# Layer 2 attention of a four-layer kernel: probabilities turned in 32x32 blocks by VectorE, value products in four row tiles, one batch behind the scores

## The chip, the core and the metric

The kernel runs on one core of one Trainium2 chip as one program. The metric is the device time of that program in microseconds (us), median over runs. TensorE (PE) multiplies matrices into PSUM, which has 8 banks; VectorE (DVE), ScalarE (ACT) and GpSimd (POOL) work element by element; SyncE (SP) issues the DMA transfers. The engines run their own instruction streams in program order and wait for each other by semaphores.

## What is computed

The program is a stack of four layers, each an attention over a context of 1500 rows and a feed-forward part. Only the attention of the third (numbered 2) is changed. Its reference, with 16 batches, 56 queries, 1500 context rows, 16 heads of 64:

```python
xn = _ln(x, ln1_s, ln1_b);  cn = _ln(context, lnc_s, lnc_b)
q = xn @ Wq
k, v = jnp.split(cn @ Wkv, 2, axis=-1)
k = jnp.concatenate((nk, k), axis=2)      # one null key and one null value in front
v = jnp.concatenate((nv, v), axis=2)
sim = jnp.where(mfull, jnp.einsum('bhid,bhjd->bhij', q * scale, k), max_neg)
attn = jax.nn.softmax(sim, axis=-1)
out = jnp.einsum('bhij,bhjd->bhid', attn, v)
out = out.transpose(0, 2, 1, 3).reshape(b, n, h * d) @ Wo
return _ln(out, lno_s, lno_b)
```

## The kernel before

All of the stage is float32. The weights are folded first, so that queries and values meet the normalised context itself: `QZ` holds per batch 16 heads x 56 queries = 896 query rows of 128 features, which are seven **tiles** of 128 rows (`RT = 7`), 112 tiles in all. The 128th feature row stands for the null key. The context lies in 12 chunks of 125 rows (`NCH`, `CH`).

For a tile m of batch b = m // 7 the work is a chain over four engines:

- PE, `scores(m, c)`, line 1611: three products of the tile with 501 keys each, into three of six PSUM banks, two tiles in turn.
- DVE, `maximum(m)`, line 1823: adds the mask `MA`, takes the row maximum and writes the sum to SBUF (`SM`).
- ACT, `exp(m)`, line 1751: exponential into `PR` with the row sums. DVE, `scale(m)`, lines 1830 and 1832: reciprocal of the sum, and `PR` times it.
- PE, `unit("T", m, j)`, line 1625: twelve transposes of 126 columns, four to a bank, in the last two banks in turn; three copies take them to SBUF as `PT` (DVE line 1800, ACT line 1740).
- PE, `unit("O", m, 0)`, line 1630: twelve products of a 125-key chunk of `V` with 128 columns of `PT`, summed in one bank; ACT copies the result over the tile's rows in `QZ` (line 1742).

The order is written out by hand in each engine's loop over n: `scores(n + 2, c)` stand between the three groups of transposes of tile n, and the value products of tile n-1 behind them. `WideHeadUnits` numbers these units and gives each of them its bank and the copy it has to wait for.

Once per batch the keys of the next one are loaded transposed (`load_keys`), together with their means and scales spread over all partitions, and POOL normalises them in place (lines 1725 and 1728). The keys of batch 0 come from PE transposes instead (line 1638). The values are loaded plain (`RAW`), and DVE normalises them in twelve instructions (line 1813). ACT makes the next batch's mask (line 1758). After the last tile the products with `WVO` follow (line 1704), a layer norm and the residual sum.

Two short pieces of other stages are read in the prediction: line 498, the value products of layers 0 and 3, which already run in four column tiles (`tile_position=(0, 32 * g)`: 128 input rows, 32 output rows each), and line 1044, a product with 56 input rows between products with 125 and 112 (lines 1043 and 1033).

Of the kernel before, what the change touches and what calls it, by code (L numbers as in the profile page):

```python
# [8 lines left out]
U8 = mybir.dt.uint8  # L9
# [4 lines left out]
P = 128  # L14
# [1380 lines left out]
RT = 7  # L1395
NPR = 501


class WideAhead:
# [3 lines left out]
    SEMS = "w_loaded rows_loaded products scaled centred summed ve_ready spread"  # L1403

    def __init__(self, ctx, nc, k, src):
# [5 lines left out]
        self.WORK = sb("work", [P, 2, 2, 2048])  # L1411
# [4 lines left out]
        self.W = self.WORK[0:HD].rearrange("p a b n -> p (a b) n").rearrange("p m (h n) -> p m h n", h=H)  # L1416
# [30 lines left out]
    def variances(self):  # L1447
        self.nc.vector.tensor_scalar(self.rs[:], self.k.ctx_mv[:, :, :, 1], 1e-6, None, ALU.add).then_inc(self.s.ve_ready, 1)
# [12 lines left out]
class WideHeadUnits:  # L1461


    def __init__(self):
        self.units = [("K", 0, j, "D") for j in range(3)]
        self.last_step = RT * B + 1
        for n in range(self.last_step + 1):
            self.units += [u for u in (self.first(n), self.second(n), self.third(n), self.output(n)) if u]
        self.place = {u[:3]: i for i, u in enumerate(self.units)}
        self.count = []  # L1470
        seen = {"A": 0, "D": 0}
        for u in self.units:
            seen[u[3]] += 1
            self.count.append(seen[u[3]])

    def first(self, n):
        return ("T", n, 0, "D") if n < RT * B else None

    def second(self, n):
        return ("T", n, 1, "A") if n < RT * B else None  # L1480

    def third(self, n):
        return ("T", n, 2, "A") if n < RT * B else None

    def output(self, n):
        return ("O", n - 1, 0, "A") if 0 <= n - 1 < RT * B else None

    def filled(self, *what):
        return self.place[what] + 1

    def bank(self, *what):
        return 6 + self.place[what] % 2

    def emptied(self, *what):
        i = self.place[what]
        return self.units[i][3], self.count[i]

    def before(self, *what):
        i = self.place[what] - 2
        return (self.units[i][3], self.count[i]) if i >= 0 else None  # L1500


def attention_16_wide_heads(nc, k, src, ahead):
# [7 lines left out]
    D, A = "D", "A"  # L1511
    plan = WideHeadUnits()
    with ExitStack() as ctx:
# [3 lines left out]
                       "ctx_loaded0 ctx_loaded1 mask_loaded0 mask_loaded1 null_rows constants mask_ready "  # L1517
                       "v_ready moments_filled moments_ready moments_stored slot_ready key_parts keys_moved keys_scaled filled emptied_a emptied_d scores_filled max_done exp_done rinv_ready scaled out_filled out_ready "
                       "dve_chain")
        s2 = semaphores(ctx, nc, name + "o", LN_SEMS)  # L1520
        ctx_loaded = (s.ctx_loaded0, s.ctx_loaded1)
        mask_loaded = (s.mask_loaded0, s.mask_loaded1)
# [5 lines left out]
        RAW = sb("raw", [CH, 2, NCH, P])  # L1528
        V = sb("values", [CH + 1, 2, NCH, P])
        KT = sb("keys", [P, 2, S2 + 1])  # L1530
        MR = sb("mask", [P, 2, S2], U8)
        MA = sb("maskadd", [P, 2, 3, NPR])
        PT = sb("probsT", [CH + 1, 2, NCH, P])
        OUT = sb("out", [P, TOK])
        MOMENTS = sb("moments", [B // 2 * NCH, 4, CH])
# [5 lines left out]
        SCALE_OF = WQK[:].rearrange("p h n -> p (h n)")[:, 0:S2]  # L1541
        PR = WORK[:, 0].rearrange("p a n -> p (a n)")[:, 0:2 * 3 * NPR].rearrange("p (u n) -> p u n", u=2)
        SM = WORK[:, 1].rearrange("p a n -> p (a n)")[:, 0:2 * 3 * NPR].rearrange("p (u n) -> p u n", u=2)
        tile_rows = lambda m: QZ[:, m // RT, m % RT * P:(m % RT + 1) * P]
        heads_of = lambda b, h: QZ[:, b, h * Q:(h + 1) * Q]
        half = lambda x, h: QZ[:, 8 * x:8 * x + 8, h * Q:(h + 1) * Q]
        keys_in = lambda c: CH + 1 if c == NCH - 1 else CH

        def wait_emptied(eng, which):
            e, n = which  # L1550
            eng.wait_ge(s.emptied_a if e == A else s.emptied_d, n)

        def wait_context(eng, b):
            eng.wait_ge(ctx_loaded[b % 2], 16 * (b // 2 + 1))

        def wait_mask(eng, b):
            eng.wait_ge(mask_loaded[b % 2], 16 * (b // 2 + 1))
# [4 lines left out]
        def _(sp):  # L1562
            def load_context(b):
                if b >= 2:
                    sp.wait_ge(s.v_ready, 3 * b - 3)
                sp.dma_start(RAW[:, b % 2], src["ctx"][b]).then_inc(ctx_loaded[b % 2], 16)

            def load_mask(b):
                if b >= 2:
                    sp.wait_ge(s.mask_ready, b - 1)  # L1570
                sp.dma_start(MR[:, b % 2, :], src["mask_full"][b].partition_broadcast(P)).then_inc(mask_loaded[b % 2], 16)

            load_context(0)
            for u in range(2):
                sp.dma_start(V[CH:CH + 1, u, NCH - 1, :], k.ident[P - 1:P, :]).then_inc(s.null_rows, 16)
            def load_keys(b):
                if b == 1:
                    sp.wait_ge(s.slot_ready, 2)
                    sp.wait_ge(s.q_filled, 2 * H)
# [1117 lines left out]
```

## Time and profile before

| | us |
|---|---|
| median of 3 runs | 2212.78 (2210.36 to 2214.6) |
| span of the profiled execution | 2210.2 |
| layer 2 attention, first scores to the products with `WVO` | 896.5 to 1636.5 |
| PE busy over the span | 2062.2 (93%) |
| DVE, ACT, POOL busy over the span | 1482.6, 1200.2, 752.7 |

The profile is of one execution, whose span runs from its first to its last instruction; the runs have no such span, so the median is set beside it. A float32 product shows in the trace as two records, each with a weight load of its own: called passes here; a transpose is one. PE's records overlap, since products are pipelined: how long one occupies the engine is read from the distance between starts, not from its duration.

### The profile page before, as it was taken

What the parts mean: (1) busy time and instruction counts of PE and PEld (TensorE: products, weight loads), DVE (VectorE), ACT (ScalarE), POOL (GpSimd) and SP (SyncE); (2) the same over time, 40 slices, a digit from 0 to 9 for tenths busy, and PEclk for the clock granted to TensorE, in tenths of its full rate; (3) what the DMA queues carried; (4) which work ended last, traced back from release to release, by engine and by line L of the source; (5) the groups of instructions that cost most, each with busy time, mean ns of one, the idle gap of its engine ahead of it and who ended that gap; (6) DMA issues with size and microseconds to landing.
All of it is one profiled execution on the core that took longest, in us unless ns stands there. A gap on an engine that the chain in (4) does not pass through costs nothing. (4 is left out here: it accounts for less than half of the span.)

```text
span 2210.2 us, 47308 instructions
## 1 busy us (share of the span) xinstructions
PE 2062.2 (93%) x18797; PEld 1505.9 (68%) x18797; DVE 1482.6 (67%) x3068; ACT 1200.2 (54%) x2313; POOL 752.7 (34%) x337
## 2 busy tenths in 40 slices
PE   5999999866999899999999999999997799999996
PEld 3677777655887455677777777777764457777774
DVE  5677777688986554566666666666626577777774
ACT  5877887634766222344444444444421467777763
POOL 6565566016875470112111211112000254433410
PEclk8999999967999898999999999999997889999997
DMA  6554544233540311231112211131000354544420
GB/s 161 148 148 132 159 134 132 63 85 97 143 136 20 79 38 39 70 104 66 60 60 82 97 60 60 60 100 62 1 1 25 87 159 126 149 126 139 122 79 9
DMA packets 94541, 199.78 MB, mean 90 GB/s; under 512 B 42113, under 2 KB 50353, under 8 KB 94066
## 3 DMA queue, kind: packets, MB, share of 16 engines
q1 hardware_dynamic: 94322, 196.75, 30.3%
q8 instruction: 151, 2.47, 0.5%
q14 instruction: 68, 0.56, 0.1%
HBM read 116.22 MB, written 0.65 MB: 53 GB/s over the span
## 5 line engine op out<-in xcount | busy, mean ns | idle before, releaser
L1630 PEld LDWEIGHTS L2ps<-L2probsT,L2values 125*128 125x128 f32 (+1 forms) x2688 | 317.4, 192 | 51.3 <-issue 48.9
L1611 PE MATMUL L2ps<-L2keys,L2qz 128*128 128x501 f32 x672 | 340.2, 590 | 0.9 <-DVE L2out_bias L1847 0.9
L1630 PE MATMUL L2ps<-L2probsT,L2values 125*128 125x128 f32 (+1 forms) x2688 | 318.5, 275 | 0.5 <-ACT L2probsT L1740 0.5
L1725 POOL TENSOR_TENSOR L2keys<-L2keys,L2mean_spread 127x1500 f32<-127x1500 f32 x15 | 50.9, 3395 | 583.0 <-DMA L2wqk<-L_moments 583.0
L1823 DVE CUSTOM_DVE_ANT_0 L2work<-L2ps,L2maskadd,L2big 128x1503 f32<-128x1503 f32 x112 | 199.5, 1781 | 72.9 <-PE L2ps L1611 72.7
L1625 PEld LDWEIGHTS L2ps<-const,L2work 128*126 128x126 f32 x1344 | 164.3, 140 | 118.7 <-issue 116.5
L654 ACT ACTIVATE L3probsT<-L3ps 128x448 f32<-128x448 f32 x384 | 196.0, 547 | 71.1 <-PE L3ps L511 66.5
L654 ACT ACTIVATE L0probsT<-L0ps 128x448 f32<-128x448 f32 x384 | 198.1, 551 | 47.7 <-PE L0ps L511 46.6
L1625 PE MATMUL L2ps<-const,L2work 128*126 128x128 f32 x1344 | 202.8, 273 | 3.5 <-DVE L2work L1832 3.1
L1742 ACT COPY L2qz<-L2ps 128x128 f32<-128x128 f32 x112 | 29.7, 265 | 304.7 <-PE L2ps L1630 304.7
L798 DVE TENSOR_REDUCE L0partmax<-L0ps 112x1 f32<-112x1000 f32 x128 | 153.4, 1199 | 58.1 <-PE L0ps L484 56.0
L798 DVE TENSOR_REDUCE L3partmax<-L3ps 112x1 f32<-112x1000 f32 x128 | 153.4, 1199 | 58.1 <-PE L3ps L484 56.0
L1751 ACT ACTIVATE L2work<-L2work,L2negmax 128x1503 f32<-128x1503 f32 x112 | 173.9, 1553 | 16.9 <-DVE L2negmax L1823 16.8
L1740 ACT COPY L2probsT<-L2ps 126x512 f32<-126x512 f32 x224 | 130.7, 585 | 77.2 <-PE L2ps L1625 77.2
L1800 DVE COPY L2probsT<-L2ps 126x512 f32<-126x512 f32 x112 | 77.4, 691 | 134.4 <-PE L2ps L1625 134.3
L511 PEld LDWEIGHTS L0ps<-L0query_stack,L0key_stack 99*128 99x128 bf16 x1536 | 110.3, 99 | 57.2 <-issue 13.3
L511 PEld LDWEIGHTS L3ps<-L3query_stack,L3key_stack 98*128 98x128 bf16 x1536 | 110.3, 99 | 54.5 <-issue 13.6
L1832 DVE TENSOR_SCALAR L2work<-L2work,L2rinv 128x1503 f32<-128x1503 f32 x112 | 138.2, 1234 | 3.9
L511 PE MATMUL L0ps<-L0query_stack,L0key_stack 99*128 99x112 bf16 x1536 | 133.5, 214 | 1.3 <-ACT L0probsT L654 1.3
L511 PE MATMUL L3ps<-L3query_stack,L3key_stack 98*128 98x112 bf16 x1536 | 133.1, 214 | 0.0
L605 POOL TENSOR_TENSOR L3keys<-L3keys,L3key_parts 128x1500 f32<-128x1500 f32 x16 | 48.5, 3034 | 192.9 <-ACT L3key_parts L701 192.9
L793 DVE TENSOR_REDUCE L0partmax<-L0ps 112x1 f32<-112x500 f32 x128 | 86.2, 674 | 33.2 <-PE L0ps L476 33.2
(479 smaller groups left out, 4164.7 us busy)
## 6 DMA issues: line engine op xcount, KB each, us to landing
L0key_stack<-L0key_parts SPq DMA_DIRECT2D x192, 187.5 KB
L3key_stack<-L3key_parts SPq DMA_DIRECT2D x192, 187.5 KB
L0ctxT<-in_ctxT SPq DMA_DIRECT2D x16, 750.0 KB, 4.4
L1rawT<-in_ctxT SPq DMA_DIRECT2D x16, 750.0 KB, 6.5
L2raw<-in_ctx SPq DMA_DIRECT2D x16, 750.0 KB
L3ctxT<-in_ctxT SPq DMA_DIRECT2D x16, 750.0 KB, 4.4
L2mean_spread<-L_moments SPq DMA_DIRECT2D x15, 750.0 KB, 6.7
L2wqk<-L_moments SPq DMA_DIRECT2D x15, 750.0 KB, 8.4
```

The lines of the kernel that those rows point to most:

```text
L511: last = nc.tensor.matmul(PS[:, bank, c * TT:(c + 1) * TT], KS[:, h % 4, tau, key_columns(4 * j + c)], QS[:, h % 4, tau, :], start=True, s ...
L654: ins = nc.scalar.activation(PT[:, h % 2, 4 * j:4 * j + 4, tau, :], PS[:, bank, 0:HALF].rearrange("p (c n) -> p c n", c=4), ACT.Exp)
L793: nc.vector.tensor_reduce(PM[:, h % 2, tau, 0:1], PS[0:TT, 0, 0:500], AX.X, ALU.max).then_inc(s.m0_done, 1)
L798: nc.vector.tensor_reduce(PM[:, h % 2, tau, 1:2], PS[0:TT, 1:3, 0:500], AX.XY, ALU.max).then_inc(s.m12_done, 1)
L1611: last = nc.tensor.matmul(PS[:, 3 * (m % 2) + c, 0:NPR], tile_rows(m), KT[:, m // RT % 2, 500 * c:500 * c + NPR], start=True, stop=True)
L1625: last = nc.tensor.transpose(PS[0:CH + 1, bank, c * P:(c + 1) * P], PR[:, i % 2, at:at + CH + 1], k.ident)
L1630: last = nc.tensor.matmul(PS[:, bank, 0:P], V[0:keys_in(c), i // RT % 2, c, :], PT[0:keys_in(c), i % 2, c, :], start=c == 0, stop=c == NCH ...
L1740: ins = nc.scalar.copy(PT[:, i % 2, 4 * j:4 * j + 4, :].rearrange("p c n -> p (c n)"), PS[0:CH + 1, bank, :])
L1751: nc.scalar.activation(PR[:, m % 2, :], SM[:, m % 2, :], ACT.Exp, bias=nmax[:, m % 4:m % 4 + 1], scale=-1.0, accum_out=ssum[:, m % 4:m % 4 ...
L1800: ins = nc.vector.tensor_copy(PT[:, i % 2, 4 * j:4 * j + 4, :].rearrange("p c n -> p (c n)"), PS[0:CH + 1, bank, :])
L1823: nc.vector.tensor_tensor_reduce(SM[:, m % 2, :].rearrange("p (c n) -> p c n", c=3), PS[:, 3 * (m % 2):3 * (m % 2) + 3, 0:NPR], MA[:, m // ...
L1832: nc.vector.tensor_scalar(PR[:, m % 2, :], PR[:, m % 2, :], rinv[:, m % 4:m % 4 + 1], None, ALU.mult).then_inc(s.scaled, 1)
```

## The change

Only `attention_16_wide_heads` and the small class `WideAhead`, which prepares for it, are touched; `WideHeadUnits` goes.

- The 1500 keys are no longer met in three runs of 501 but in four **windows** of 12 x 32: window w takes from each chunk of 125 its keys 32w to 32w+31 (`key_window`), so a row of probabilities is 48 blocks of 32 (1536 columns; those past a chunk's end are masked, and the null key has one of them). The four products of a tile fill banks 0 to 3, for all tiles from the ninth on.
- `scale` moves from DVE to ACT, `exp` works in place, and DVE turns the tile's probabilities in 32x32 blocks from SBUF to SBUF in one instruction (`turn`). So the block's 32 keys lie on the 32 partitions of the quadrant that held 32 of the tile's query rows. `PT` holds a whole batch turned.
- The value products (`weigh`) run once over a whole batch: for each of 48 blocks, four products, one on each quadrant of 32 partitions (`tile_position=(a * 32, 0)`), with 224 columns (seven tiles x 32 query rows), into banks 4 to 7. Their values `V` lie in all four quadrants, so each row is loaded four times. Seven steps of seven blocks (the last of six) stand behind the scores, eight tiles later (`LAG`). ACT empties the four banks once per batch (`take_heads`).
- The values are normalised on POOL, 12 instructions a window with means and scales from `VST`, and are single: the next batch's windows are loaded as the steps let go of them. The keys of batch 0 are loaded and normalised as all others are.

```diff
-NPR = 501
+WINDOWS = 4
+BW = 32
+BLOCKS = WINDOWS * NCH
+NPR = BLOCKS * BW
+LAG = RT + 1
...
+        score_bank = lambda m: 4 if m < LAG and m % 2 else 0
...
+            return KEYS[:, at:at + NCH * CH].rearrange("p (c n) -> p c n", n=CH)[:, :, 0:BW]
...
+            def load_values(b, w):
+                if b:
+                    last_step = (NCH * w + NCH - 1) // RT
+                    sp.wait_ge(s.pv_done, RT * (b - 1) + last_step + 1)
...
+                for a in range(4):
+                    sp.dma_start(V[a * BW:a * BW + n, w * NCH:(w + 1) * NCH, :], src["ctx"][b][w * BW:w * BW + n]
+                                 ).then_inc(values_loaded[w], 16)
...
+            for b in range(B):
+                if b + 1 < B:
+                    load_keys(b + 1)
+                    load_moments(b + 1)
+                    load_mask(b + 1)
+                if b:
+                    for w in range(WINDOWS):
+                        load_values(b, w)
...
+            def scores(m):
+                b = m // RT
+                if m > LAG:
+                    pe.wait_ge(s.max_done, m)
+                elif m >= 2:
+                    pe.wait_ge(s.max_done, m - 1)
+                if m % RT == 0:
+                    pe.wait_ge(s.keys_scaled, b + 1)
+                for w in range(WINDOWS):
+                    last = nc.tensor.matmul(PS[:, score_bank(m) + w, 0:NCH * BW], tile_rows(m), key_window(b, w), start=True, stop=True)
+                last.then_inc(s.scores_filled, 1)
+
+            def weigh(step):
+                b, g = divmod(step, RT)
+                if g == 0:
+                    pe.wait_ge(s.turned, RT * b + RT)
+                    if b:
+                        pe.wait_ge(s.heads_ready, 4 * b)
...
+                blocks = step_blocks(g)
+                pe.wait_ge(s.v_ready, WINDOWS * b + blocks[-1] // NCH + 1)
+                for n in blocks:
+                    for a in range(4):
+                        last = nc.tensor.matmul(PS[:, 4 + a, 0:RT * BW], V[a * BW:(a + 1) * BW, n, :], block_cells(a, b, n),
+                                                start=n == 0, stop=n == BLOCKS - 1, tile_position=(a * BW, 0))
+                last.then_inc(s.pv_done, 1)
...
-            for j in range(3):
-                unit("K", 0, j, D)
...
+            for n in range(1, TILES + LAG):
+                if n < TILES:
+                    scores(n)
+                if n >= LAG:
+                    weigh(n - LAG)
...
+            def normalise_values(b, w):
+                pool.wait_ge(values_loaded[w], 64 * (b + 1))
+                blocks = slice(w * NCH, (w + 1) * NCH)
+                nc.gpsimd.tensor_copy(V[:, blocks, P - 1:P], NULL[:, blocks].unsqueeze(2))
+                for c in range(NCH):
+                    x = V[:, w * NCH + c, 0:P - 1]
+                    last = nc.gpsimd.tensor_scalar(x, x, VST[:, 0, w, b, c:c + 1], VST[:, 1, w, b, c:c + 1],
+                                                   ALU.subtract, ALU.mult)
+                last.then_inc(s.v_ready, 1)
...
+            def scale(m):
+                act.wait_ge(s.rinv_ready, m + 1)
+                nc.scalar.mul(SM[:, m % 2, 0:NPR], SM[:, m % 2, 0:NPR], rinv[:, m % 4:m % 4 + 1]).then_inc(s.scaled, 1)
+
+            def take_heads(b):
+                act.wait_ge(s.pv_done, RT * b + RT)
+                for a in range(4):
+                    nc.scalar.copy(by_quadrant(b)[:, :, a, :], PS[:, 4 + a, 0:RT * BW].rearrange("p (t n) -> p t n", n=BW)
+                                   ).then_inc(s.heads_ready, 1)
...
+            for n in range(TILES + LAG):
+                b, t = divmod(n, RT)
+                if n < TILES:
+                    exp(n)
+                if n >= LAG and (n - LAG) % RT == RT - 1:
+                    take_heads((n - LAG) // RT)
+                if n < TILES:
+                    scale(n)
...
+            def turn(m):
+                b, t = divmod(m, RT)
+                dve.wait_ge(s.scaled, m + 1)
+                if b:
+                    dve.wait_ge(s.pv_done, RT * (b - 1) + t + 1)
+                nc.vector.transpose(turned_cells(b, t), SM[:, m % 2].rearrange("p (g r n) -> p g r n", g=RT, n=BW)
+                                    ).then_inc(s.turned, 1)
...
+            for n in range(TILES + 1):
+                if n < TILES:
+                    maximum(n)
+                if n:
+                    turn(n - 1)
+                if n < TILES:
+                    invert(n)
```

PE before, from the end of the folding into the loop of tiles and one period of it (`L2work` holds the probabilities, `L2values` the values or, at line 1638, the keys' source):

```order
L1676 MATMUL L2ps<-L2bias_heads,L2work 128x1 x16
L1638 MATMUL L2ps<-const,L2values 128x125 x11
L1638 MATMUL L2ps<-const,L2values 128x126
L1611 MATMUL L2ps<-L2keys,L2qz 128x501 x6
L1625 MATMUL L2ps<-const,L2work 126x128 x4
L1611 MATMUL L2ps<-L2keys,L2qz 128x501
```

PE after, at the same place (line 1615 is `scores`, line 1631 `weigh`):

```order
L1664 MATMUL L2ps<-L2work 128x128 x16
L1670 MATMUL L2ps<-L2bias_heads,L2work 128x1 x16
L1615 MATMUL L2ps<-L2keys,L2qz 128x384 x36
L1631 MATMUL L2ps<-L2work,L2values 128x224 x28
L1615 MATMUL L2ps<-L2keys,L2qz 128x384 x4
```

The transposes are gone, nine tiles of scores stand ahead of the first value products, and from there 4 products of scores and 28 of values alternate.

DVE before, one tile in the middle of a batch that has a part of the next batch's values to normalise (`ISA` is the instruction of `maximum`):

```order
L1800 COPY L2probsT<-L2ps 126x512
L1813 TENSOR_SCALAR L2values<-L2raw,ctx_mv,L2rs 125x127 x4
L1830 RECIPROCAL L2rinv<-L2sums 128x1
L1832 TENSOR_SCALAR L2work<-L2work,L2rinv 128x1503
L1823 ISA L2work,L2negmax<-L2ps,L2maskadd,L2big 128x1503
L1823 ISA L2negmax 128x1
```

DVE after, one tile (the turn is of the tile before):

```order
L1806 ISA L2work,L2negmax<-L2ps,L2maskadd,L2big 128x1536
L1806 ISA L2negmax 128x1
L1816 STREAM_TRANSPOSE L2work<-L2work 128x49x32
L1821 RECIPROCAL L2rinv<-L2sums 128x1
L1806 ISA L2work,L2negmax<-L2ps,L2maskadd,L2big 128x1536
```

The copy, the scaling and the values have left DVE; the turn has come.

POOL after, one batch (before, the first two rows were all that stood here; `L2wqk` holds the scales):

```order
L1697 TENSOR_TENSOR L2keys<-L2keys,L2mean_spread 127x1500
L1699 TENSOR_TENSOR L2keys<-L2keys,L2wqk 127x1500
L1704 COPY L2values<-L2null_column 128x12
L1707 TENSOR_SCALAR L2values<-L2values,L2value_stats 128x127 x12
L1704 COPY L2values<-L2null_column 128x12
```

The last two kinds come four times a batch, behind the keys of the next one.

## Rows read from the trace of the kernel before

**Rows 1.** Stretches: us, engines' busy us (instructions), PE clock, DMA share, GB/s.

```profile
894.00:898.00 4.00, 3.13 (x10) 1.79 (x9) 1.94 (x4) 0.00 (x0) 0.98 (x1) 0.50 0.46 169
1000.00:1100.00 100.00, 100.00 (x645) 77.26 (x644) 67.19 (x105) 47.01 (x79) 14.68 (x4) 1.00 0.20 66
```

**Rows 2.** Timeline of PE, one tile: start us, us, line, operation, count.

```profile
1203.47 2.84 PE L1630 MATMUL L2ps<-L2probsT,L2values 125*128 125x128 f32 x24
1206.15 0.60 PE L1625 MATMUL L2ps<-const,L2work 128*126 128x128 f32 x4
1206.59 1.01 PE L1611 MATMUL L2ps<-L2keys,L2qz 128*128 128x501 f32 x2
...
1209.99 2.84 PE L1630 MATMUL L2ps<-L2probsT,L2values 125*128 125x128 f32 x24
```

**Rows 3.** Groups by line, 900 to 1630: count, busy us, mean ns, idle before.

```profile
L1823 DVE CUSTOM_DVE_ANT_0 L2work<-L2ps,L2maskadd,L2big 128x1503 f32<-128x1503 f32 x112 | 199.5, 1781 | 72.9 <-PE L2ps L1611 72.7
L1751 ACT ACTIVATE L2work<-L2work,L2negmax 128x1503 f32<-128x1503 f32 x112 | 173.9, 1553 | 16.9 <-DVE L2negmax L1823 16.8
...
L1832 DVE TENSOR_SCALAR L2work<-L2work,L2rinv 128x1503 f32<-128x1503 f32 x112 | 138.2, 1234 | 3.9
L1740 ACT COPY L2probsT<-L2ps 126x512 f32<-126x512 f32 x223 | 130.1, 585 | 77.0 <-PE L2ps L1625 76.9
...
L1813 DVE TENSOR_SCALAR L2values<-L2raw,ctx_mv,L2rs 125x127 f32<-125x127 f32 x180 | 49.7, 340 | 0.0
...
L1742 ACT COPY L2qz<-L2ps 128x128 f32<-128x128 f32 x110 | 29.2, 265 | 300.1 <-PE L2ps L1630 300.1
L1758 ACT ACTIVATE L2maskadd<-L2mask,L2big 128x1500 f32<-128x1500 uint8 x15 | 23.3, 1551 | 0.0
...
L1830 DVE RECIPROCAL L2rinv<-L2sums 128x1 f32<-128x1 f32 x112 | 17.9, 160 | 48.0 <-ACT L2work L1751 47.9
```

**Rows 4.** Timeline of PE in layer 0, four column tiles and what follows.

```profile
151.84 0.78 PE L498 MATMUL L0ps<-L0probsT,L0values 128*32 128x112 f32 x24
152.55 0.42 PE L484 MATMUL L0ps<-L0key_stack,L0query_stack 97*112 97x500 bf16 x1
```

**Rows 5.** Timeline of PE in layer 1, a 56-row product between others.

```profile
575.47 2.79 PE L1043 MATMUL L1ps<-L1raw,L1probsT 125*112 125x128 f32 x24
578.19 0.47 PE L1044 MATMUL L1ps<-L1v_latents,L1probsT 56*112 56x128 f32 x2
578.59 1.56 PE L1033 MATMUL L1ps<-const,L1probs 112*125 112x112 f32 x12
579.99 0.26 PE L1036 MATMUL L1ps<-const,L1probs 112*56 112x112 f32 x1
```

**Rows 6.** Groups by line on POOL, whole span.

```profile
L609 POOL TENSOR_SCALAR L0key_parts<-L0keys 128x1500 bf16<-128x1500 f32 x15 | 59.9, 3994 | 2.9 <-POOL L0keys L605 2.9
...
L1728 POOL TENSOR_TENSOR L2keys<-L2keys,L2wqk 127x1500 f32<-127x1500 f32 x15 | 58.4, 3892 | 1.2
L1725 POOL TENSOR_TENSOR L2keys<-L2keys,L2mean_spread 127x1500 f32<-127x1500 f32 x15 | 50.9, 3395 | 583.0 <-DMA L2wqk<-L_moments 583.0
...
L1722 POOL COPY L2keys<-const 128x1 f32<-128x1 f32 x1 | 0.2, 187 | 0.1
```

**Rows 7.** Issues of transfers, 830 to 1640: count, KB each, median us to landing.

```profile
L2mean_spread<-L_moments SPq DMA_DIRECT2D x15, 750.0 KB, 6.7
```

**Rows 8.** Timeline of PE at the start of the stage.

```profile
889.47 3.63 PE L1676 MATMUL L2ps<-L2bias_heads,L2work 64*128 64x1 f32 x32
893.03 2.64 PE L1638 MATMUL L2ps<-const,L2values 125*128 125x125 f32 x12
896.54 7.12 PE L1611 MATMUL L2ps<-L2keys,L2qz 128*128 128x501 f32 x12 [0.87 <-DVE L2out_bias L1847]
```

**Rows 9.** Instructions of a line: count, ns min/median/max, first and last start.

```profile
L1823 DVE CUSTOM_DVE_ANT_0 L2work<-L2ps,L2maskadd,L2big x112: 1768/1783/1784, 901.3 to 1620.9; 128x1503 f32<-128x1503 f32 x112
L1704 PE MATMUL L2ps<-L2qz,L2wvo x64: 539/539/644, 1636.5 to 1660.3; 128*128 128x448 f32 x64
```

More of the change, by code:

```diff
@@ L1458, in vector @@
                                 ).then_inc(s.summed, 1)
[L1461 to L1500, printed above, removed]
 def attention_16_wide_heads(nc, k, src, ahead):
@@ L1527, in attention_16_wide_heads @@
         BIG = sb("big", [P, 1])
[L1528 to L1535, printed above, removed]
+        V = sb("values", [P, BLOCKS, P])
+        NULL = sb("null_column", [P, BLOCKS])
+        VST = sb("value_stats", [P, 2, WINDOWS, B, NCH])
+        KEYS = sb("keys", [P, 2 * KEY_COLUMNS + (WINDOWS - 1) * BW - 3])
+        MR = sb("mask", [P, S2], U8)
+        MA = sb("maskadd", [P, 2, WINDOWS, NCH, BW])
         MEAN = sb("mean_spread", [P, S2])
@@ L1549, in wait_emptied @@
[L1549 to L1557, printed above, removed]
+        by_quadrant = lambda b: QZ[:, b].rearrange("p (t a n) -> p t a n", a=4, n=BW)
+        score_bank = lambda m: 4 if m < LAG and m % 2 else 0
+        KT = KEYS[:, 0:2 * KEY_COLUMNS].rearrange("p (u n) -> p u n", u=2)
@@ L1593, in _ @@
             sp.wait_ge(s.moments_stored, 16)
-            load_keys(1)
-            for b in range(2, B):
-                load_context(b)
-                load_mask(b)
-                load_keys(b)
+            load_moments(0)
+            for x, of in enumerate((ahead.means, rs)):
+                for w in range(WINDOWS):
+                    n = BW if w < WINDOWS - 1 else LAST_KEYS
+                    for a in range(4):
+                        sp.dma_start(VST[a * BW:a * BW + n, x, w], of[w * BW:w * BW + n]).then_inc(s.stats_spread, 16)
@@ new lines, in _ @@
+            nc.gpsimd.memset(BIG[:], FLT_MAX).then_inc(s.constants, 1)
+            for u in range(2):
+                nc.gpsimd.memset(MA[:, u, WINDOWS - 1, :, LAST_KEYS:BW], FLT_MAX).then_inc(s.margins, 1)
+            for u in range(2):
+                pool.wait_ge(s.margins, u + 1)
+                nc.gpsimd.memset(MA[:, u, WINDOWS - 1, NCH - 1, LAST_KEYS:LAST_KEYS + 1], 0.0).then_inc(s.margins, 1)
+            pool.wait_ge(s.margins, 4)
+            normalise_keys(0)
+            pool.wait_ge(s.stats_spread, 16 * 2 * WINDOWS * 4)
@@ L1730, in _ @@
+            pool.wait_ge(s.null_column, 2)
+            pool.wait_ge(s.null_rows, 64)
+            for b in range(B):
+                if b + 1 < B:
+                    normalise_keys(b + 1)
+                for w in range(WINDOWS):
+                    normalise_values(b, w)
             ln_pool(pool, k, s2)
```

298 lines of the change are left out of this document (114 added, 184 removed).

## The prediction

> **What bounds the kernel now.** I read the table of stretches first. In the middle of the stage [rows 1] PE is busy for all of the 100 us at a granted clock of 1.00 (2.4 GHz), VectorE for 67, ScalarE for 47, POOL for 15: nothing keeps PE waiting, so the stage lasts as long as PE's instructions do. The timeline of PE gives the period of a tile [rows 2]: value products begin at 1203.47 and again at 1209.99, 6.52 us. Of this the 24 value passes take 2.68 (1203.47 to 1206.15), three groups of four transposes 0.44 each (1206.15 to 1206.59), and three pairs of score passes the rest, 2.52, so 0.84 a pair. 112 periods are 730 of the stage's 740 us. The groups by line say what the others do in a period [rows 3]: DVE 1.78 for the maximum, 1.23 for the scaling, 0.16 for the reciprocal; ACT 1.55 for the exponential.
>
> **PE after.** A pass of 128 columns takes 2.68/24 = 0.1117 us, one of 501 columns 0.42 [rows 2]; the line through both is 0.0059 + 0.000827 per column. So a pass of 384 columns takes 0.323, and the eight of a tile's scores 2.59 (before 2.52). One of 224 columns takes 0.191. The twelve transposes (1.32) go, and nothing else on PE waited for them.
>
> A step of value products is 28 products, 56 passes: 14 rounds of four row tiles. If four tiles run side by side, a round takes 0.191 and a step 2.67; the seventh step of a batch, with six blocks, 2.29. Row tiles aren't in this trace; the nearest are column tiles [rows 4]: 24 passes of 112 columns take 0.71 us to the start of what follows. One after the other, at 0.0985 each by the line, they would take 2.36, so a round costs 0.118 or less. I take full overlap, since this is the nearest row, and keep no overlap (0.764 a round) as the far end.
>
> Going into tiles and out again costs something too. In layer 1 [rows 5] two products of 56 rows stand between wider ones: from 575.47 to 579.99 are 38 passes in 4.52 us, which at 0.110 each would be 4.18, so 0.34 for in and out. From the column tiles it would be 0.71 - 6 x 0.0985 = 0.12. I take 0.35 a step. The period is 2.59 + 2.67 + 0.35 = 5.61 us, 5.23 with the short step, 5.56 on the mean, and 38.9 a batch.
>
> **DVE and ACT.** `maximum` grows from 1503 to 1536 columns, 1.82 us [rows 3]. The copy (0.69) and the scaling go. `turn` is not in the trace: 1568 columns, SBUF to SBUF. At the rate of the scaling it takes 1.29, at that of the maximum 1.86, at twice that 3.7. I take 1.86, the slower of the two that show. With 0.16 for the reciprocal a tile costs DVE some 3.95 us with gaps. ACT has the exponential 1.59, the scaling, a pass of the same length, 1.59, a seventh of a mask (1.55) and of four copies of 224 columns. A copy of 512 takes 0.585, one of 128 0.265 [rows 3], so one of 224 takes 0.345, four 1.4: some 3.6 with gaps. Both lie under 5.56.
>
> The waits: `scores(n+1)` wants `maximum(n)`, 1.82 after the scores, which the step of 3.0 covers. `turn(n-1)` waits for `weigh(n-8)`, since it writes over the cells which that step has read; behind it queue `invert(n)` and `maximum(n+1)`. It starts when the step ends and takes 1.86 + 0.16 while PE does scores for 2.59: 0.6 to spare. The banks 4 to 7 are emptied when the last step of a batch ends; ACT begins when its exponential is done, 1.82 + 1.78 after the scores' end, and copies until 5.0, where PE wants the banks at 5.2. That has the least slack; if it fails, a few tenths a batch are lost, 5 us in all.
>
> **POOL, SP and transfers.** Per batch POOL has the keys, 3.40 + 3.89 [rows 6] and a little, 7.4, and now 48 normalisations of 127 columns and four small copies (0.2). Line 609, the same operation on 1500 columns, takes 3.99, 2.66 ns a column, so 0.34 for 127; a small instruction costs 0.19 [rows 6]. I take 0.53. The bounds are 0.25 (the rate of line 1725 and nothing more) and 0.87 (a pass for each of its two operations). At 0.53 a batch costs 7.4 + 4 x (0.2 + 12 x 0.53) = 33.6 us, under 38.9, so PE hides it; from 0.64 a normalisation POOL is the bound. The Trainium skill, "GPSIMD Engine Reference", section 4.1 Engine selection, calls GpSimd roughly line-rate on operations with one tensor input and about two times slower than VectorE on those with two. By that a normalisation would take what it takes DVE at line 1813, 0.34 [rows 3], and POOL 24.5 us a batch; line 609 has one tensor input and takes more for a column than line 1725 with two, so here the row speaks against the page, and I keep 0.53.
>
> Values are now loaded four times, 3.1 MB a batch, and 5.6 MB in all: 144 GB/s over 38.9 us where 66 are moved now at a DMA share of 0.20 [rows 1]. A window is let go by a step of one batch and needed by the same step of the next or one before, over 27 us later; its loading takes some 7 [rows 7] and its normalising 6.6. SP issues 21 transfers a batch in place of 6. So I cost these at nothing; the cover is those 27 us. The keys of the next batch stand on SP behind the last window of the batch before, and on POOL behind its normalisation, and are still done well inside the batch.
>
> **Start and end.** Without the transposes of the keys the first scores begin at 893.0, not 896.5 [rows 8]. The clock there is 0.50, 1.2 GHz [rows 1]: six passes of 501 until the first maximum at 901.3 [rows 9] took 4.76, so eight of 384 take 4.86, and the first maximum starts at 897.9. Until the first value step, eight tiles later, DVE is the bound at 3.95 a tile: `maximum(7)` starts at 925.5 and ends at 927.4, `turn(6)` ends at 929.3, `weigh(0)` at 932.3. If the clock stays at 0.50 here, PE takes 5.2 a tile and 7 us are lost. Then 103 periods of 5.556 end at 1504.8. The last tile's turn ends at 1510.3 (scores, maximum, exponential, scaling, turn in a row), the last batch's 96 rounds take 18.3 more, the copies 1.4, and the products with `WVO` start at about 1530.5 where they start at 1636.5 now [rows 9]. That is 106 us less: span 2104.2. The median of the runs is 2.6 above the span of the profiled execution, so **2107**. Its own range, from a switch of 0.12 (-26) with a turn of 1.29 at the start (-5), to a lost clock, late copies and tile starts of some hundredths a round, is 2075 to 2135.
>
> **The rivals.**
> - Weight loads of the four row tiles queue up, and the kernel is **slower**. Each product loads 128 columns of weights. The 32 passes with one column [rows 8] take 0.111 us each, so a load is a floor of 0.111, hidden today behind a pass of the same length. Four in a row are 0.444 a round where columns need 0.191. The column tiles don't exclude it: their loads are of 32 columns, and four of a quarter are one of 0.111, within the 0.118 seen. Against it: loads for different rows of the array need not share anything. A batch would take 7 x 2.59 + 96 x 0.444 + 2.45 = 63.2 us, 14.7 batches 357 more, the tail 24: 2488. It decides from a round of 0.26 us, since 1507 rounds (15.7 batches) by 0.07 are the 106 us. Chance 0.14.
> - Tiles overlap less than fully. At a round of 0.25, a third over the columns' time, 1507 x 0.058 = 88: 2195. The Trainium skill, "TensorE: Matmul & The Clock Gate", section Measured speedup vs the span model, has four row tiles of 32 rows at 3.07 times one; by that a round is 0.191 x 4 / 3.07 = 0.249, the same 2195. Rows 4 show more than that for column tiles: 2.36 / 0.71 = 3.3 with the exit included. Chance 0.14.
> - POOL becomes the bound. At 0.87 a batch costs 50 us, 16 of them 800, and the products start near 1701: 2280. From 0.78 it is slower than now. Chance 0.09, of which 0.05 slower.
> - The turn takes 3.7. DVE needs 5.8 a tile, 0.24 over PE, and 15 more at the start: 2150. Chance 0.05.
> - The change doesn't do what it says, and the four row tiles run one after the other: a step is 56 x 0.191 = 10.7, a batch 93.9, some 2970. Chance 0.05.
>
> **How the numbers follow.** The forecast keeps 0.53. About 0.2% is what a measurement of this kernel can tell from no change. Faster: 0.53 + 0.14 + 0.05 + 0.04, less 0.02 for cases that end near the old time, 0.74; slower 0.14 + 0.05 + 0.05 = 0.24. The range reaches from 2075 to POOL's 2280 and leaves out queued loads and no overlap, 0.19.
>
> **What would show it.** In a stretch in the middle PE should be busy throughout, with tiles 5.56 us apart; in a step four passes should start within hundredths of each other and rounds 0.19 apart. A round of 0.44 means queued loads; 0.76 no overlap. POOL should idle some 5 us a batch, `turn` take 1.9 and wait for PE; the first maximum should start near 898 and the products with `WVO` near 1530. PE waiting for values means POOL; PE waiting for the maximum means DVE.

## The result and the profile after

The changed kernel takes 2521.93 us (median of 4 runs, 2518.67 to 2526.13) where the kernel before takes 2213.69 in the same job: 1.1398 times as long, interval 1.138 to 1.1415. The forecast was 2107, in a range of 2075 to 2280. The span of the profiled execution is 2524.3 us.

The products with `WVO` (line 1684 now) begin at 1949.9, where they began at 1636.5 [rows 9]; so all of the loss lies in the stage, as it did in the sum:

```profile
L1684 PE MATMUL L2ps<-L2qz,L2wvo x64: 539/539/643, 1949.9 to 1973.7; 128*128 128x448 f32 x64
```

PE's timeline in the middle of it (start, us, line, operation, count) first shows what was forecast, then a hole:

```profile
1394.51 2.92 PE L1615 MATMUL L2ps<-L2keys,L2qz 128*128 128x384 f32 x8
1397.36 2.93 PE L1631 MATMUL L2ps<-L2work,L2values 32*128 32x224 f32 x56
1400.22 2.92 PE L1615 MATMUL L2ps<-L2keys,L2qz 128*128 128x384 f32 x8
1403.07 2.93 PE L1631 MATMUL L2ps<-L2work,L2values 32*128 32x224 f32 x56
1430.50 4.65 PE L1615 MATMUL L2ps<-L2keys,L2qz 128*128 128x384 f32 x8 [24.50 <-DVE L2negmax L1806]
1435.09 2.93 PE L1631 MATMUL L2ps<-L2work,L2values 32*128 32x224 f32 x56
```

The scores take 2.85 us (1394.51 to 1397.36), the step of values 2.86 (to 1400.22), a tile 5.71. Then, behind the step at 1403.07, PE stands for 24.50 us and comes back at half clock (granted 0.50 from 1431 to 1432): the scores take 4.59. Such a hole comes about once a batch. What PE waited for in the stage (us in total, times, longest):

```profile
PE L2ps L1615 <- DVE L2negmax L1806: 329.8, 16, 25.5
PE L2ps L1631 <- POOL L2values L1707: 36.1, 7, 12.6
PE L2ps L1631 <- DVE L2work L1816: 4.9, 2, 3.2
```

The maximum on DVE is only the last in a row of waits. It stands on DVE behind the reciprocal of the tile before (line 1821 below, idle for 352.1 us), that waits for the exponential on ACT, and ACT stands at the mask of the next batch. So the prediction's sign "PE waiting for the maximum means DVE" misleads here: DVE is busy for only 31.5 of the 100 us from 1400 to 1500. ACT's waits, and its timeline beside PE's hole:

```profile
ACT L2maskadd L1762 <- DMA L2mask<-in_mask_full: 358.3, 14, 28.0
```

```profile
1425.17 1.26 ACT L1762 ACTIVATE L2maskadd<-L2mask,L2big 128x1152 f32<-128x1152 uint8 x1 [26.99 <-DMA L2mask<-in_mask_full]
...
1426.83 1.55 ACT L1744 ACTIVATE L2work<-L2work,L2negmax 128x1536 f32<-128x1536 f32 x1
```

The mask is wanted in the third tile of a batch for the one after, five tiles before its first use, but ACT's stream is in order, and the exponential of the fourth tile stands behind it. So the question is why the mask is late. SP's issues between two batches (the second number is from the issue to SP's next):

```profile
1449.11 3.83 SPq L1552 DMA_DIRECT2D L2values<-in_ctx  x4
1452.98 8.72 SPq L1566 DMA_DIRECT2D L2keys<-in_ctxT  x2
1461.74 0.77 SPq L1574 DMA_DIRECT2D L2mean_spread<-L_moments  x1
1462.55 2.68 SPq L1574 DMA_DIRECT2D L2wqk<-L_moments  x1
1465.27 3.07 SPq L1558 DMA_DIRECT2D L2mask<-in_mask_full  x1
```

The mask goes out 16 us after the last window's values, and lands late on top of that. Issues in the stage, with KB each and the median us to landing:

```profile
L2values<-in_ctx SPq DMA_DIRECT2D x166, 192.0 KB, 3.5
L2wqk<-L_moments SPq DMA_DIRECT2D x13, 750.0 KB, 27.5
L2values<-in_ctx SPq DMA_DIRECT2D x52, 174.0 KB
L2mean_spread<-L_moments SPq DMA_DIRECT2D x12, 750.0 KB, 7.7
L2keys<-in_ctxT SPq DMA_DIRECT2D x12, 656.2 KB, 11.6
L2mask<-in_mask_full SPq DMA_DIRECT2D x13, 187.5 KB, 25.4
L2keys<-in_ctxT SPq DMA_DIRECT2D x12, 87.9 KB, 27.5
```

25 us for 187.5 KB, while 192 KB of values land in 3.5. (The two loads of the keys share a semaphore, and so do means and scales, so the second of a pair tells when both are there.) And the transfers are not short of bandwidth. Stretches (busy time of each engine, then PE's clock, the mean busy share of the 16 DMA engines, GB/s):

```profile
1406.00:1430.50 24.50, 0.00 (x1) 0.00 (x0) 2.00 (x4) 4.89 (x6) 11.30 (x14) 0.59 0.27 77
1450.00:1459.00 9.00, 9.00 (x102) 6.25 (x104) 6.10 (x7) 5.92 (x10) 9.00 (x13) 1.00 0.07 27
1462.00:1468.00 6.00, 6.00 (x66) 4.18 (x65) 3.99 (x5) 1.57 (x1) 1.92 (x3) 1.00 1.03 290
1482.00:1494.00 12.00, 0.00 (x0) 0.00 (x0) 0.00 (x0) 2.64 (x3) 8.57 (x12) 0.50 0.06 26
```

While loads are queued, from 1450 to 1459 and again from 1482 to 1494, the share is 0.06 to 0.07, as much as one engine of sixteen, at 26 to 27 GB/s. Between them, the same queue reaches 290. What keeps one engine busy, the first four runs below did not ask; they went at the mask and at POOL.

The other engines, by line over the stage:

```profile
L1707 POOL TENSOR_SCALAR L2values<-L2values,L2value_stats 128x127 f32<-128x127 f32 x768 | 617.1, 847 | 0.0
...
L1806 DVE CUSTOM_DVE_ANT_0 L2work<-L2ps,L2maskadd,L2big 128x1536 f32<-128x1536 f32 x112 | 203.6, 1818 | 119.1 <-PE L2ps L1615 119.1
L1816 DVE STREAM_TRANSPOSE L2work<-L2work 128x1568 f32<-128x1568 f32 x112 | 202.7, 1810 | 123.1 <-PE L2ps L1631 121.5 <-ACT L2work L1749 1.6
L1749 ACT ACTIVATE L2work<-L2work,L2rinv 128x1536 f32<-128x1536 f32 x112 | 176.8, 1579 | 116.9 <-DVE L2rinv L1821 116.9
...
L1754 ACT COPY L2qz<-L2ps 128x224 f32<-128x224 f32 x64 | 17.1, 349 | 45.3 <-PE L2ps L1631 45.3
L1821 DVE RECIPROCAL L2rinv<-L2sums 128x1 f32<-128x1 f32 x112 | 14.9, 133 | 352.3 <-ACT L2work L1744 352.1
```

### The profile page after: what moved, and what is told of

Same layout as the page of the kernel before. It is cut to its first block and busy times, and to the rows that moved or that the text cites. A ratio compares the mean times of both kernels' runs of the same rounds, so it can differ in the third digit from the quotient of the medians.

```text
span 2524.3 us, 52181 instructions
## 1 busy us (share of the span) xinstructions
PE 2008.6 (80%) x21121; PEld 1411.6 (56%) x21121; DVE 1418.6 (56%) x2765; ACT 1258.0 (50%) x2169; POOL 1368.9 (54%) x1176
## 5 line engine op out<-in xcount | busy, mean ns | idle before, releaser
L1615 PE MATMUL L2ps<-L2keys,L2qz 128*128 128x384 f32 x896 | 360.2, 549 | 330.5 <-DVE L2negmax L1806 329.8
L1707 POOL TENSOR_SCALAR L2values<-L2values,L2value_stats 128x127 f32<-128x127 f32 x768 | 617.1, 847 | 0.0
L1615 PEld LDWEIGHTS L2ps<-L2keys,L2qz 128*128 128x128 f32 x896 | 176.3, 207 | 474.9 <-DVE L2negmax L1806 336.9
L1631 PE MATMUL L2ps<-L2work,L2values 32*128 32x224 f32 x6144 | 334.5, 365 | 41.0 <-POOL L2values L1707 36.1
L1631 PEld LDWEIGHTS L2ps<-L2work,L2values 32*128 32x128 f32 x6144 | 295.4, 192 | 106.3 <-issue 58.8
L1816 DVE STREAM_TRANSPOSE L2work<-L2work 128x1568 f32<-128x1568 f32 x112 | 202.7, 1810 | 123.1 <-PE L2ps L1631 121.5
L1806 DVE CUSTOM_DVE_ANT_0 L2work<-L2ps,L2maskadd,L2big 128x1536 f32<-128x1536 f32 x112 | 203.6, 1818 | 119.1 <-PE L2ps L1615 119.1
L1744 ACT ACTIVATE L2work<-L2work,L2negmax 128x1536 f32<-128x1536 f32 x112 | 176.2, 1573 | 134.9 <-DVE L2negmax L1806 134.7
L1749 ACT ACTIVATE L2work<-L2work,L2rinv 128x1536 f32<-128x1536 f32 x112 | 176.8, 1579 | 116.9 <-DVE L2rinv L1821 116.9
L1821 DVE RECIPROCAL L2rinv<-L2sums 128x1 f32<-128x1 f32 x112 | 14.9, 133 | 352.3 <-ACT L2work L1744 352.1
L1762 ACT ACTIVATE L2maskadd<-L2mask,L2big 128x1152 f32<-128x1152 uint8 x16 | 20.2, 1264 | 358.3 <-DMA L2mask<-in_mask_full 358.3
L605 POOL TENSOR_TENSOR L3keys<-L3keys,L3key_parts 128x1500 f32<-128x1500 f32 x16 | 48.6, 3035 | 195.5 <-ACT L3key_parts L701 195.5
L605 POOL TENSOR_TENSOR L0keys<-L0keys,L0key_parts 128x1500 f32<-128x1500 f32 x16 | 48.6, 3037 | 130.2 <-ACT L0key_parts L701 130.2
## 6 DMA issues: line engine op xcount, KB each, us to landing
L0key_stack<-L0key_parts SPq DMA_DIRECT2D x192, 187.5 KB
L3key_stack<-L3key_parts SPq DMA_DIRECT2D x192, 187.5 KB
```

The costliest lines, as they stand in the source:

```text
L605: nc.gpsimd.tensor_tensor(x, x, parts[:, 0], ALU.subtract).then_inc(s.parts_ready, 1)
L1615: last = nc.tensor.matmul(PS[:, score_bank(m) + w, 0:NCH * BW], tile_rows(m), key_window(b, w), start=True, stop=True)
L1631: last = nc.tensor.matmul(PS[:, 4 + a, 0:RT * BW], V[a * BW:(a + 1) * BW, n, :], block_cells(a, b, n), start=n == 0, stop=n == BLOCKS - 1, ...
L1707: last = nc.gpsimd.tensor_scalar(x, x, VST[:, 0, w, b, c:c + 1], VST[:, 1, w, b, c:c + 1], ALU.subtract, ALU.mult)
L1744: nc.scalar.activation(SM[:, m % 2, 0:NPR], SM[:, m % 2, 0:NPR], ACT.Exp, bias=nmax[:, m % 4:m % 4 + 1], scale=-1.0, accum_out=ssum[:, m % ...
L1749: nc.scalar.mul(SM[:, m % 2, 0:NPR], SM[:, m % 2, 0:NPR], rinv[:, m % 4:m % 4 + 1]).then_inc(s.scaled, 1)
```

## The experiments

**Is it the mask or POOL?** The theory then: ACT stands at the mask, because its load is issued too late on SP and lands 25 us after. The rival: POOL, whose normalising takes 0.80 us (9.61 for twelve), and whose 46 us a batch are more than PE's 39.6. The first run moves the mask's load ahead:

```diff
+            load_mask(1)
             for b in range(B):
                 if b + 1 < B:
                     load_keys(b + 1)
                     load_moments(b + 1)
-                    load_mask(b + 1)
                 if b:
-                    for w in range(WINDOWS):
+                    for w in range(2):
                         load_values(b, w)
+                if b + 2 < B:
+                    load_mask(b + 2)
+                if b:
+                    for w in range(2, WINDOWS):
+                        load_values(b, w)
```

> One part moved: the load of the next batch's mask goes ahead on SP, between two windows of values one batch earlier, where what it waits for is long done; all else as in the changed kernel. Theory (the queue): ScalarE stands 25 us a batch at the mask, because its transfer is issued behind keys, means and scales and lands 25 us after its issue; so the stall goes, 15 x 25 = 375 us at most, and what is late next is POOL, 4 x (0.2 + 12 x 0.80) + 6 to 7 = 46 us a batch where PE needs 39.6: about 2524 - 16 x 20 = 2200, between 2150 and 2290. Rival (POOL): the values' normalising holds the loop already, the mask is late only because the steps are, and the time stays within 2% of 2522.

Measured: 2410.2 us, 1.0882 times the kernel before (1.086 to 1.0904). The wait for the mask is gone but for the first, 8.4 us. Yet only 112 us came back, not 320, so neither the theory's number nor the rival's holds. PE now waits for values and keys:

```profile
PE L2ps L1636 <- POOL L2values L1712: 188.0, 46, 11.8
PE L2ps L1620 <- POOL L2keys L1704: 16.4, 15, 1.9
```

The second run leaves out POOL's normalising, so its values stay as loaded, and keeps SP's order.

```diff
-                nc.gpsimd.tensor_copy(V[:, blocks, P - 1:P], NULL[:, blocks].unsqueeze(2))
-                for c in range(NCH):
-                    x = V[:, w * NCH + c, 0:P - 1]
-                    last = nc.gpsimd.tensor_scalar(x, x, VST[:, 0, w, b, c:c + 1], VST[:, 1, w, b, c:c + 1],
-                                                   ALU.subtract, ALU.mult)
-                last.then_inc(s.v_ready, 1)
+                nc.gpsimd.tensor_copy(V[:, blocks, P - 1:P], NULL[:, blocks].unsqueeze(2)).then_inc(s.v_ready, 1)
```

> The 48 normalising instructions of a batch are left out (the values stay as loaded; the copy of the null column gives the signal), the order on SP is that of the changed kernel. Theory (the queue): POOL idles 20 us of 66 a batch already, so the stall at the mask stays at some 20 to 25 us a batch and only the end of the stage gets shorter, by the 33 us that PE waited there for POOL: 2440 to 2510. Rival (POOL): without its 39 us a batch the loop falls to PE's 39.6 a batch, 2100 to 2150.

Measured: 2500.72 us in one run, as the theory had it. With 38 of POOL's 46 us a batch gone the time falls by 1%, and ACT waits for the mask as before:

```profile
ACT L2maskadd L1757 <- DMA L2mask<-in_mask_full: 374.3, 14, 27.6
```

So POOL does not hold the loop, in spite of its price. The third run moves the other end of the wait, where ACT makes the mask.

```diff
-                if t == 2 and b + 1 < B:
+                if t == 5 and b + 1 < B:
```

> ScalarE makes the next batch's mask after tile 5 of a batch and not after tile 2; SP's order is that of the changed kernel. Theory (the queue): the mask is wanted three periods (3 x 5.70 = 17 us) later, so 17 of the 25 us a batch go, 15 x 17 = 257 less: about 2270, and not under 2200, where POOL's 46 us a batch stand. Rival (POOL): no change, within 2% of 2522.

Measured: 2417.95 us in one run. The direction is the theory's, the size is not: the wait for the mask falls from 358.3 to 50.5 us, but PE waits 192.5 for values and 38.3 for keys instead. From either end, the mask is worth 104 to 112 us, and something else stands right behind it.

The fourth takes the mask early, as in the first run, and the normalising in two operations a window (shown here):

```diff
...
-                for c in range(NCH):
-                    x = V[:, w * NCH + c, 0:P - 1]
-                    last = nc.gpsimd.tensor_scalar(x, x, VST[:, 0, w, b, c:c + 1], VST[:, 1, w, b, c:c + 1],
-                                                   ALU.subtract, ALU.mult)
-                last.then_inc(s.v_ready, 1)
+                x = V[:, blocks, 0:P - 1]
+                of = lambda k: VST[:, k, w, b].unsqueeze(2).to_broadcast([P, NCH, P - 1])
+                nc.gpsimd.tensor_tensor(x, x, of(0), ALU.subtract).then_inc(s.v_moved, 1)
+                pool.wait_ge(s.v_moved, WINDOWS * b + w + 1)
+                nc.gpsimd.tensor_tensor(x, x, of(1), ALU.mult).then_inc(s.v_ready, 1)
```

> The mask's load early as in the first run, and the values of a window normalised by two operations of 12 x 127 columns with means and scales spread by a zero stride, in place of twelve of 127 with two scalars each. The same kind took 3.1 us for 1500 columns at the keys, so 6.4 a window, 26 a batch and 32 with the keys. Theory: POOL falls under PE's 39.6 us a batch and PE is the bound: 2524 - 15 x 27 = about 2120, 2095 to 2160, faster than the kernel before (2213). Rival: the keys' transfers, which land 10 to 28 us after their issue, become the next wait, some 5 to 10 us a batch: 2200 to 2280.

Measured: 2340.49 us, 1.0576 times the kernel before (1.055 to 1.0601). Both numbers missed again. POOL's price fell from 9.6 to 5.5 us a window, and POOL waits where PE's steps need the last window:

```profile
1361.84 2.73 POOL L1714 TENSOR_TENSOR L2values<-L2values,L2value_stats 128x1524 f32<-128x1524 f32 x1
1389.03 0.20 POOL L1709 COPY L2values<-L2null_column 128x12 f32<-128x12 f32 x1 [24.45 <-DMA L2values<-in_ctx]
```

The fourth window's values are issued on SP before 1357 (when the next keys' issue begins) and are there at 1389: over 30 us, where the loads of the other windows land in 3.5. What sets this window apart is 29 rows in place of 32. That was the second theory: **a transfer of 29 rows runs on one DMA engine**. Four of them are 4 x 29 x 6144 bytes = 0.71 MB, at 27 GB/s some 26 us (an estimate), and keys, means, scales and mask, each with a share on that engine, land behind them. Against it: the values are loaded four times, and the queues are simply full.

The fifth run cuts the 29 rows and changes nothing else in the changed kernel, but that POOL waits for the count of eight transfers; the sixth loads 28 of them, in one transfer a quadrant (`LAST_KEYS - 1` in place of `LAST_KEYS` in the first line below).

```diff
-                n = BW if w < WINDOWS - 1 else LAST_KEYS
+                parts = ((0, BW),) if w < WINDOWS - 1 else ((0, 16), (16, LAST_KEYS))
                 for a in range(4):
-                    sp.dma_start(V[a * BW:a * BW + n, w * NCH:(w + 1) * NCH, :], src["ctx"][b][w * BW:w * BW + n]
-                                 ).then_inc(values_loaded[w], 16)
+                    for i, j in parts:
+                        sp.dma_start(V[a * BW + i:a * BW + j, w * NCH:(w + 1) * NCH, :], src["ctx"][b][w * BW + i:w * BW + j]
+                                     ).then_inc(values_loaded[w], 16)
...
-                pool.wait_ge(values_loaded[w], 64 * (b + 1))
+                pool.wait_ge(values_loaded[w], (64 if w < WINDOWS - 1 else 128) * (b + 1))
```

> The changed kernel with one edit: the four loads of the last window (29 rows each) are issued as 16 rows and 13 rows; order, bytes and all other engines stay. Theory (one DMA engine): a transfer of 29 rows runs on one of the 16 DMA engines, at 26 to 28 GB/s with 1.05 engines busy, so the four take 25 us and every later transfer has a share queued behind them; split, they land in 3 to 6 us, the mask about 10 us after its issue, and the wait of ScalarE for it falls from 24 to under 5 us a batch. Then POOL's 46 to 48 us a batch are the bound: 2524 - 15 x 19 = about 2235, between 2180 and 2290. Rival (bytes and issues): the transfers are late because values are loaded four times in many issues; four more issues a batch change nothing or cost 1 to 2 us a batch, 2510 to 2560.

> The changed kernel, but the last window loads 28 of its 29 rows (the 29th key of each chunk's last window keeps value zero), in as many issues and 3% fewer bytes. Theory (one DMA engine): 28 rows are spread over several engines where 29 were not, so the time falls as with the split: 2180 to 2290. Rival (bytes and issues): 2500 to 2525.

Measured: 2199.7 us with the cut, 0.9953 of the kernel before (0.9935 to 0.9971), and 2205.91 in one run with 28 rows. With four more transfers a batch the kernel is 322 us faster, and with 3% fewer bytes in that one window it is 316 faster: the rival is out. The landings with the cut:

```profile
L2wqk<-L_moments SPq DMA_DIRECT2D x11, 750.0 KB, 9.3
L2keys<-in_ctxT SPq DMA_DIRECT2D x11, 656.2 KB, 6.2
...
L2mask<-in_mask_full SPq DMA_DIRECT2D x11, 187.5 KB, 9.2
L2keys<-in_ctxT SPq DMA_DIRECT2D x11, 87.9 KB, 6.7
```

Scales, mask and the small part of the keys fall from 25 to 28 us to 7 to 9, and the mask is in time where the changed kernel has it. What holds this kernel is POOL, as a stretch and the waits of PE show:

```profile
1200.00:1300.00 100.00, 90.49 (x960) 64.12 (x964) 55.41 (x61) 53.63 (x59) 99.84 (x122) 0.95 0.49 135
```

```profile
PE L2ps L1632 <- POOL L2values L1708: 39.4, 15, 3.9
```

**Both together.** The cut, the mask early, the two spread operations:

> The split of the last window's loads, the mask's load early, and the values normalised by two spread operations a window. Theory: with no transfer on a single engine and POOL at 4 x 5.6 + 6 = 29 us a batch, nothing is later than PE, whose period is 5.70 (39.5 a batch): 2340 - 15 x (53 - 39.6) = 2140, less some 10 at the end of the stage: 2105 to 2150, faster than the kernel before (2213). Rival (bytes and issues): it stays at the 2340 of the same kernel without the split.

Measured: 2114.88 us, 0.9556 of the kernel before (0.9539 to 0.9572). In the middle PE is busy throughout at full clock:

```profile
1200.00:1300.00 100.00, 100.00 (x1106) 69.42 (x1100) 64.79 (x72) 63.27 (x70) 71.12 (x35) 1.00 0.62 153
```

```profile
L1690 PE MATMUL L2ps<-L2qz,L2wvo x64: 539/539/643, 1542.9 to 1566.6; 128*128 128x448 f32 x64
```

Between 950 and 1500 PE waits for nothing. The next run has the cut and the two operations with the mask where the changed kernel has it:

> The split and the cheap normalising, with the mask's load where the changed kernel has it, behind keys and means. Theory: the mask is then issued some 5 us after the last window's loads and lands about 12 us later, near the time when ScalarE wants it, so 0 to 5 us a batch are lost against the run with the mask early: 2110 to 2220. Rival (order on SP): the place behind keys and means is enough to stall ScalarE by 10 us or more a batch, 2270 or above.

Measured: 2121.82 us in one run. ACT waits 26.0 us for the mask over the stage. With the cut, the mask's place on SP is worth some 7 us and not 112; the four runs of the kernel with the mask early spread over 9 (2110.04 to 2118.93), so the 7 are hardly clear of them.

**Is it the number of rows?** The fastest kernel with its cut moved:

```diff
-                parts = ((0, BW),) if w < WINDOWS - 1 else ((0, 16), (16, LAST_KEYS))
+                parts = ((0, BW),) if w < WINDOWS - 1 else ((0, 23), (23, LAST_KEYS))
```

> As the fastest run so far (split, mask early, two spread operations a window), but the 29 rows of the last window are cut into 23 and 6 in place of 16 and 13: the same bytes in as many issues. Theory (the engines that a transfer runs on are as many, up to 16, as divide its rows): 23 rows fall on one engine again, 4 x 23 x 6144 bytes at 27 GB/s are 21 us where 29 rows were 27, so most of the loss comes back: 2340 - 15 x 6 = 2250, between 2170 and 2340. Rival (a transfer of more than 16 rows that is no multiple of 16 is slow only as a whole, and any cut mends it): 2105 to 2130, as with 16 and 13.

Measured: 2273.34 us in one run, 158 slower than with 16 and 13. The scales land 27.5 us after their issue again:

```profile
L2wqk<-L_moments SPq DMA_DIRECT2D x10, 750.0 KB, 27.5
...
L2mask<-in_mask_full SPq DMA_DIRECT2D x10, 187.5 KB, 17.0
```

```profile
1352.00:1362.00 10.00, 3.51 (x36) 3.34 (x40) 1.39 (x2) 1.96 (x3) 9.10 (x5) 0.67 0.07 28
```

The last row is a stretch after the last window's loads, columns as above. So cutting as such doesn't help; 28, 16 and 13 rows are fast, 29 and 23 slow. The Trainium skill, "DMA: Bandwidth & Descriptors", section Why a DMA increments its semaphore by 16 and not by 1, gives the rule: a transfer runs on the largest number of engines, up to 16, that divides the size of the slowest dimension on both sides. By it 28 rows get 14, 16 rows 16, 13 rows 13, 29 and 23 rows one. The traces agree: a share of 0.06 to 0.07 and 27 GB/s at 29 rows, 0.07 and 28 at 23, and short landings with 28, 16 and 13.

The number of engines stands in no row, but the pages of the profile count packets. In this order, 29 rows (the changed kernel), 28, 16 and 13 (the cut alone), 23 and 6:

```profile
DMA packets 105520, 240.03 MB, mean 95 GB/s; under 512 B 45689, under 2 KB 54929, under 8 KB 105025
DMA packets 106287, 239.64 MB, mean 109 GB/s; under 512 B 46520, under 2 KB 55760, under 8 KB 105792
DMA packets 107312, 240.04 MB, mean 109 GB/s; under 512 B 47480, under 2 KB 56720, under 8 KB 106816
DMA packets 105899, 239.99 MB, mean 106 GB/s; under 512 B 46072, under 2 KB 55312, under 8 KB 105408
```

A program has 64 of these loads, four in each of 16 batches. Against 29 rows the packets under 512 B are 831, 1791 and 383 more, so 13, 28 and 6 a load; the mask's place and the two operations do not change the count (47480 with all three as well). If every engine of a transfer adds one small packet, which is read from the fit and not shown by itself, and 29 rows have one, then 28 rows have 14, 16 and 13 rows 29, and 23 and 6 rows 7: the rule's numbers.

The page also says that the lowest-numbered engines are taken; by that every other transfer would have a share on the busy one. No run here shows an engine's number, but the single packets in the trace of the changed kernel show such a share: of the 128 packets of the mask that SP issued at 1399.70, 120 start between 1403.4 and 1405.1, and the last eight, a sixteenth, one after another between 1424.2 and 1424.6. ACT, which waits for all of them, goes on at 1425.17.

The last run leaves the normalising out of the kernel with cut and early mask.

> Split and mask early, with the normalising of the values left out altogether (the values stay as loaded). Theory: with two spread operations a window POOL is already hidden and PE is the bound, so the time is that of the run with them, 2105 to 2125. Rival (some of POOL's work is still waited for, or slows VectorE and the transfers while it runs): 2060 to 2100.

Measured: 2110.41 us in one run, inside the spread of the kernel with the two operations (2110.04 to 2118.93): POOL's 29 us a batch are hidden, and PE is the bound.

## Why the prediction was wrong

**The step that failed** is the one on POOL, SP and transfers: "So I cost these at nothing; the cover is those 27 us", with "its loading takes some 7". That 7 was the landing of a transfer of 128 partitions [rows 7], put in place of four of 29. These need some 26 us of one engine by the estimate above, and landed some 35 us after their issue (SP from 1383.22, POOL goes on at 1419.20), so past the cover. And it wasn't the values alone that paid: scales and mask, which SP issued next, landed 25 to 28 us after their issue. The bytes were summed (144 GB/s), but not the engines that carry them. The same sentence passed over the mask. Its load was moved behind keys, means and scales and its buffer halved, ACT wants it in tile 2 of a batch, and the text named the queue without asking who at the far end of it stands in order. Cutting the 29 rows gives back 322 of the 415 us that the forecast missed.

The stall's price follows from the rows. From the first scores to the products with `WVO` this kernel takes 406 us longer than the one with nothing late (spans 2524.3 and 2117.1). PE waits 372.7 us there, 329.8 of them for the maximum and 36.1 for POOL, against 12.2, and is busy for 681.5 us with the same products, against 636.1. The 45 us more go with a lower granted clock (0.81 over the stage against 0.99): a tile after a hole takes some 1.7 to 2.9 us longer.

**The rival that came near the number was not what happened.** Queued weight loads would have given 2488; the four row tiles run side by side. The 56 passes of a step start in groups of four within 0.02 us, and the groups follow each other at 0.189 us, forecast 0.191. The rival of less overlap (0.25 a round) fell with it. That 2488 lies near the measured 2522 is chance.

**POOL** is a second term that was mis-sized. It was priced at 0.53 a normalising and kept to 0.87 above; it took 0.80. At that price POOL is the bound, as the prediction had it from 0.64 on: the run with the cut alone has POOL at 99.84 of 100 us and a batch of 46, and takes 2199.7 us. The POOL rival's own sum gives 2226 with 0.80 in place of 0.87, and the keys, at 6.3 us a batch in place of 7.4, are some 18 us of the rest. So this term stands for some 78 us (2199.7 to 2121.82, the mask in its place), and 2199.7 is still within the range. An estimate from this run: at 0.80 it is 12 us under the kernel before, and 48 x 14.7 normalisings by 0.017 are 12 us, so by itself POOL makes the kernel slower only from some 0.82. The prediction had 0.78. Line 609 did not tell the price, because it isn't the same operation, as the prediction says: it has one scalar operation where a normalising has two. The upper bound, one pass for each, came near; whether POOL makes two passes no run shows. The lower bound of 0.25 is not line 1725's rate either, which gives 0.29 (3395 ns x 127 / 1500). The same work as two operations of 1524 columns took 2.74 each, 5.5 for a window in place of 9.6.

**The rest of the sum held.** `maximum` took 1.82, `turn` 1.81 (forecast 1.86), the scaling on ACT 1.58 (1.59), a copy of 224 columns 0.349 (0.345) [rows 3 for those of before]. The period was 5.70, forecast 5.61: the switch into tiles and out costs 0.2 each way, some 0.4 and not 0.35, and a pass of 384 columns takes 0.330, not 0.323. (The rows of layer 1 had said so: with 26 passes of 128 columns at 0.1117 and 12 of 112 at 0.0985, in place of 38 at 0.110, in and out come to 0.43 there and not 0.34.) In the kernel with nothing late the first step of values starts at 930.95 (929.3 forecast as the start, with 932.3 its end) and the products with `WVO` at 1542.9 (1530.5): 103 periods by 0.1 are 10 of these 12. Its 2114.9 is 0.4% over the forecast. But that kernel has the two-operation normalising, which the change did not have; with the transfers alone set right it is 2199.7, 4.4% over. So the forecast held for PE, VectorE and ScalarE, and missed what 29 rows did to the transfers and, by less, what POOL takes.

## What to carry to other kernels

Ask of every transfer that a change adds into how many rows it falls and how many engines those give, before adding up bytes; here a ragged last piece (29 of 32 rows) cost 322 us, and loading it as 16 and 13 is a small edit. When a transfer lands late, look at the share of busy DMA engines beside it: 0.06 with a full queue was one engine of sixteen here, and not a lack of bandwidth: the same queue reached 290 GB/s between. And follow a moved load to the engine that waits for it in program order: what stands behind that wait pays, however early the data itself is wanted.

## What was not expected of the hardware

- A transfer of 29 rows runs at 26 to 27 GB/s, with 0.06 to 0.07 of the engines busy; mask and scales on the same queue then land 25 to 28 us after their issue. With the cut they land in 9.
- SP stands too while those loads are under way, and why is not shown: the two issues of the keys took 8.72 us together after the four loads of 29 rows, 0.82 for the same two in the kernel with the cut, the early mask and the two operations:

```profile
1209.99 0.82 SPq L1567 DMA_DIRECT2D L2keys<-in_ctxT  x2
```

- On GpSimd an operation of 127 columns with two scalars takes 0.80 us, about what 440 columns of the spread two-tensor operation take (2.74 for 1524).
- After a stall of 24 us PE's first eight score passes took 4.6 to 5.5 us in place of 2.85; the clock in the stretch of the stall was 0.50 to 0.59.
